# Cross-attention and expert layer on one core: head projections at tiles 4, 6, 8 and 10, the maxima turned at tile 11 behind the scores, the query jobs right behind the last scores

## What is computed

```python
def _L0_xattn_ref(x, context, Wq, Wk, Wv, Wo, bo):      # x (16, 256, 128), context (16, 1601, 96)
    q = (x @ Wq).reshape(B, Nq, HEADS, DIM_HEAD).transpose(0, 2, 1, 3)       # HEADS 16, DIM_HEAD 64
    k = (context @ Wk).reshape(B, Nc, HEADS, DIM_HEAD).transpose(0, 2, 1, 3)
    v = (context @ Wv).reshape(B, Nc, HEADS, DIM_HEAD).transpose(0, 2, 1, 3)
    sim = jnp.einsum('bhid,bhjd->bhij', q, k) * SCALE
    attn = jax.nn.softmax(sim, axis=-1)
    out = jnp.einsum('bhij,bhjd->bhid', attn, v)
    out = out.transpose(0, 2, 1, 3).reshape(B, Nq, HEADS * DIM_HEAD)
    return out @ Wo + bo
...
x = x + _L0_xattn_ref(_layernorm(x, axis=-1), ctx_768, Wq, Wk, Wv, Wo, bo)
x = x + _L0_ffn_ref(_layernorm(x, axis=-1), router, experts, shared expert)
```

## Time and profile before

| what | value |
| --- | --- |
| median of 3 runs | 3302.86 us (3302.56 to 3302.99) |
| the profiled execution | 3302.1 us, of which the trace's span is 3300.3 us |
| TensorE busy | 3269.1 us, 99% of the span |
| VectorE busy | 2383.1 us, 72% |
| ScalarE busy | 1938.2 us, 59% |
| GpSimd busy | 1069.6 us, 32% |
| first scores of the attention, start | 38.19 us |
| first expert matmul, start | 2967.16 us |

### The profile page before, as it was taken

The page is one execution under the profiler, slowest core; times in us unless marked ns, Lnnn a source line. Parts: engine busy times, 40 slices in busy tenths (PEclk is TensorE's granted clock), DMA queues, the critical chain, the costliest instruction groups (busy, mean ns, idle before and its releaser), DMA issues.

```text
span 3300.3 us, 40940 instructions
## 1 busy us (share of the span) xinstructions
PE 3269.1 (99%) x15518; PEld 2606.8 (79%) x15518; DVE 2383.1 (72%) x4915; ACT 1938.2 (59%) x2236; POOL 1069.6 (32%) x710
## 2 busy tenths in 40 slices
PE   8999999999999999999999999999999999999999
PEld 6777777777787777877777777777777877777887
DVE  6777777777777777777777777777777777777655
ACT  4565555655556555665556655566655666575554
POOL 4322233222332233322233222322223322225555
PEclk9999999999999999999999999999999999999999
DMA  2000000000000000000000000000000001000000
GB/s 79 1 16 1 16 1 11 6 1 16 1 16 1 16 1 16 1 1 16 1 16 1 16 1 16 1 9 8 1 16 1 16 1 39 1 3 4 7 7 10
DMA packets 8055, 32.39 MB, mean 10 GB/s; under 512 B 1585, under 2 KB 2354, under 8 KB 7474
## 3 DMA queue, kind: packets, MB, share of 16 engines
q1 hardware_dynamic: 7858, 29.78, 2.9%
HBM read 27.41 MB, written 2.10 MB: 9 GB/s over the span
## 4 chain that ended last, share of the span: by engine, by line
PE 98%; DVE 1%; issue 0%; ACT 0%; DMA 0%; POOL 0%; POOLq 0%; DVEq 0%; ACTq 0%
PE st L529 12%; PE st L532 12%; PE st L535 12%; PE op L543 12%; PE op L549 12%; PE op L546 12%; PE side L475 11%; PE side L555 3%; PE st L636 2%; PE st L638 2%; PE st L637 2%; PE side L468 1%; PE side L470 1%; PE side L469 1%; PE op L636 1%; PE op L637 1%
## 5 line engine op out<-in xcount | busy, mean ns | idle before, releaser
L796 ACT ACTIVATE p_full<-st 128x1024 f32<-128x1024 f32 (+1 forms) x832 | 853.8, 1026 | 1128.5 <-PE st L535 1128.4
L1061 DVE TENSOR_REDUCE m_part<-side 128x1 f32<-128x402 f32 x2016 | 1078.2, 571 | 550.6 <-PE side L475 550.6
L410 POOL TENSOR_TENSOR p_lo<-p_full,p_hi 128x1024 fp32r<-128x1024 f32 x256 | 669.2, 2614 | 2063.7 <-ACT p_hi L799 2063.7
L799 ACT ACTIVATE p_hi<-st 128x1024 fp32r<-128x1024 f32 (+1 forms) x832 | 848.6, 1020 | 0.0
L1049 DVE TENSOR_TENSOR p_lo<-p_full,p_hi 128x1024 fp32r<-128x1024 f32 (+1 forms) x576 | 700.3, 1216 | 132.7 <-ACT p_hi L799 132.7
L475 PE MATMUL side<-cT_hi,qT_hi 96*128 96x402 f32 x2016 | 555.2, 346 | 0.0
L529 PE MATMUL st<-qT_hi,cT_hi 97*128 97x512 f32 (+1 forms) x1664 | 538.4, 405 | 2.3 <-DMA qT_hi<-m_row 2.3
L543 PE MATMUL op<-p_hi,v_hi 128*97 128x512 f32 (+1 forms) x1664 | 527.1, 398 | 0.5 <-DVE p_lo L1049 0.5
L532 PE MATMUL st<-qT_lo,cT_hi 96*128 96x512 f32 (+1 forms) x1664 | 524.8, 397 | 0.0
L535 PE MATMUL st<-qT_hi,cT_lo 96*128 96x512 f32 (+1 forms) x1664 | 521.9, 395 | 0.0
L549 PE MATMUL op<-p_hi,v_lo 128*97 128x512 f32 (+1 forms) x1664 | 521.1, 394 | 0.0
(11 more groups left out here) (164 smaller groups left out, 2606.0 us busy)
## 6 DMA issues: line engine op xcount, KB each, us to landing
keys_nat<-in_ctx_keys SPq DMA_DIRECT2D x16, 624.0 KB, 5.8
keys_tur<-in_ctx_turned SPq DMA_DIRECT2D x16, 603.0 KB, 4.9
gud_raw<-in_moe_w SPq DMA_DIRECT2D x2, 1152.0 KB, 7.8
out_x<-x SPq DMA_DIRECT2D x8, 256.0 KB, 2.0
x<-in_x SPq DMA_DIRECT2D x1, 1920.0 KB, 12.1
qT_hi<-m_row SPq DMA_DIRECT2D x64, 4.0 KB
aw<-in_attn_w SPq DMA_DIRECT2D x2, 448.0 KB, 5.3
aw<-in_attn_w SPq DMA_DIRECT2D x1, 896.0 KB, 9.3
```

What stands on the lines that cost most here:

```text
L410: pool.tensor_tensor(p_lo[:, slot(s), :], p_full[:, s % 2, :], p_hi[:, slot(s), :].bitcast(F32), ALU.subtract).then_inc(s_lo_pool, 1)
L796: act.activation(p_full[0:m, s % 2, :], both(st[0:m, s % 2]), ACT.Exp, scale=SCALE)
L799: act.activation(p_hi[0:m, slot(s), :], both(st[0:m, s % 2]), ACT.Exp, scale=SCALE).then_inc(s_ex, 1)
L1061: dve.tensor_reduce(m_part[:, at:at + 1], where[:, 0:MAXW], AX.X, ALU.max).then_inc(s_drain, 1)
```

## The change

Three Y jobs move away from tile 11. One stands now behind the four M of tile 4, one behind those of tile 6, one behind those of tile 10; the one at tile 8 stays. T moves from behind `pv(9)` to ahead of it, right behind `qk(11)`. The two Q move from behind `pv(10)` to ahead of it, right behind `qk(12)`, and since one table serves all engines, `queries_lo` on VectorE moves ahead of `lo(11)` and `lo(12)`. N moves from tile 6 to tile 7. The numbers of the jobs, and so their banks and wait values, follow from the table. No instruction is added or taken away.

```diff
-        PLACES = {2: ("MM", "M"), 3: ("MM", "M"), 4: ("MM", "MM"), 5: ("MM", "M"), 6: ("MM", "MM"),
-                  7: ("MM", "MM"), 8: ("MM", "MY"), 9: ("MM", "MM"), 10: ("MM", "MM"), 11: ("YY", "YT"),
-                  12: ("", "QQ")}
-        EXTRA = {2: {5: "L", 6: "N"}, 3: {5: "R"}}
+        PLACES = {2: ("MM", "M"), 3: ("MM", "M"), 4: ("MM", "MMY"), 5: ("MM", "M"), 6: ("MM", "MMY"),
+                  7: ("MM", "MM"), 8: ("MM", "MY"), 9: ("MM", "MM"), 10: ("MM", "MMY"), 11: ("T", ""),
+                  12: ("QQ", "")}
+        EXTRA = {2: {5: "L", 7: "N"}, 3: {5: "R"}}
```

## The result

| | median | runs |
| --- | --- | --- |
| before | 3302.71 us | 3298.80 to 3302.99 |
| changed | 3685.10 us | 3675.04 to 3691.81 |

The changed kernel is slower: ratio 1.1158, with a 95% interval from 1.1127 to 1.1190. The forecast was 3592 us in a range of 3555 to 3630, so the direction was right and the size was not: 93 us more came than the forecast, and the time lies outside the range. Its runs also scatter over 17 us, where those of before scatter over 4. The profiled execution took 3691.81 us, of which the span is 3690.0 us.

The account below looks back on a forecast made before the run. TensorE, busy 99% of the span, was taken as the bound, so only new waits count: 132.3 + 5.4 + 151.9 = 289.6 us on the profiled 3302.1 us, giving a median of 3592 us, 8.8% slower, range 3555 to 3630.

Parts of the forecast that it names:

- bank waits: Head projections (Y) behind two M at tiles 4, 6, 10 wait for a bank's drain: 0.70 us each, 132.3 us.
- N: Turn moved from tile 6 to tile 7 starts 0.34 us later behind its M, 16 times: 5.4 us.
- The long wait: TensorE at pv(11) waits for tile 11's remainder, behind the queries' remainders on VectorE: 2.45 us in 62 groups, 151.9 us.
- T: Moved ahead of pv(9) at tile 11: its inputs are ready and its row goes out earlier, so it costs nothing.
- the number of runs of fp32 jobs: Five runs of fp32 jobs end per group instead of three; claimed to cost nothing that the rows show.
- One sign: In the changed trace TensorE's busy time stays near 3269 us while the span grows, its share falling to about 92%.
- the clock falls: Rival, 8%: TensorE's idle piece in each of 62 groups lowers the clock, 2.6 us lost each, 161 us more: 3753 us.
- the rival's dearer case: Clock rival (8%) with 3.4 us instead of 2.6 us lost at each of 62 long waits: 3803 us.
- Not slower: Rival, 2%: head projections find VectorE done, queries' remainder is over in time, N's waits go too: 3292 us, 0.3% faster.
- one wait missing: Rival, 4%: either tile 11's remainder is in time (3441 us) or the third job finds its bank free (3455).
- doesn't do what it says: Rival, 1%: the change doesn't do what it says; the built order was held to show that it does.

Follow-up runs that it names:

- the needless matmuls: Changed kernel plus eight needless 512-column matmuls on TensorE between pv(10) and pv(11), inside the wait for tile 11's remainder: 3596.42 us, ratio 1.0895.
- the copies early: Changed kernel with ScalarE's two copies of the queries ahead of the exponentials of tile 12 instead of behind them: 3534.14 us, ratio 1.0704.

## Why the prediction was wrong

**The waits: right.** That TensorE had no waits to save, and that the change brings 189 bank waits, 16 longer turns and 62 waits for the remainder of tile 11, is what the trace of the changed kernel shows, with these counts. The sum was 289.6 us; with a clock kept up by the needless matmuls it measured 295.

- The bank waits were sized at 0.70 us, the value of the turn, and measured 0.75. The forecast's upper end named the reason: weights of L555 behind the wait take longer to come in than those of L442. 132.3 us became 142.
- N was sized at 0.34 us more, and its idle weight-load time grew by 5.8 us in 16, 0.36 each.
- The long wait was sized at 2.45 us and measured 2.37: 151.9 us became 147. Its chain met each start within 0.02 us.
- T and the number of runs of fp32 jobs cost nothing that could be seen.
- One sign failed without the clock: TensorE's busy time was to stay near 3269 us, but a matmul behind a wait is recorded longer, and with the copies early, where every wait is there and the clock stays up, it is 3332.3 us. The share of "about 92%" would be 91% by the forecast's own numbers (3269 of 3592).

**The step that failed** is the judgement "the clock falls (8%)". Of the 93 us over the forecast 89 are the clock (3685.1 - 3596.4), and the range was closed at 3630 to leave that rival out. Two arguments carried it. The first was that the expert layer kept the clock at 1.00 with 4.1 us of idling in 25. But these were pieces of about a microsecond, like those of the kernel with the copies early, which keeps its clock as well. They say nothing of a piece twice as long. The trace of before had two such pieces, of 2.11 and 2.33 us, one right behind the other at the start of the attention:

```profile
35.58 0.27 PE L479 MATMUL side<-ident,m_neg 128*8 128x128 f32 x1 [2.11 <-DVE m_neg L920]
38.19 1.20 PE L529 MATMUL st<-qT_hi,cT_hi 97*128 97x512 f32 x2 [2.33 <-DMA qT_hi<-m_row]
```

```profile
36.34:38.19 1.85, 0.00 (x1) 0.04 (x1) 0.97 (x2) 0.00 (x0) 0.00 (x0) 0.50 0.01 2
```

The clock fell at 36.34 us, 0.5 us into the second of them, so the idling ahead of the second had its part in it, and it stayed down for 6.8 us (half of that is the 3.4 us of the rival's dearer case). This was the only evidence of the right size, no clean case of a lone piece, and it spoke for the rival. The second argument was that each new piece "stands alone among work without gaps"; the trace shows that this doesn't protect: the clock falls with TensorE busy at full pace on both sides.

The rival as it was priced, 3753 us, was too dear in its turn. It let the clock fall behind each of 62 waits, 2.6 us lost a time. In the profiled execution it fell behind 45, and (3691.8 - 3596.7) / 45 = 2.1 us were lost a time. So the truth lay between the two cases, where the range had nothing. The Trainium skill ("TensorE: Matmul & The Clock Gate", on HAM oscillation) says that idle gaps between bursts send the clock down again and again, once per gap; its example has gaps of 3 to 5 us. The trace agrees as to the kind, and differs in two things: gaps of 2.15 us are enough here, and 45 of 62 brought a fall, not every one.

**Not slower, one wait missing, doesn't do what it says**: none of it came.

## What to carry to other kernels

When a change puts an engine's wait on the matrix engine's path, price the wait and the clock apart, and take the clock's price from idle pieces of the same length; where the trace has none, keep the range open up to it. A job that stands third in a row on two banks waits for the first one's drain, wherever it stands, so put such jobs behind a single fill: here that alone made a kernel 11 us faster, by putting 16 jobs behind one M in place of two. One table that orders all engines moves the waits of each of them; what the moving engine gains nothing by, another may pay for, and its order can be kept apart.

## What the runs showed of the hardware

- Needless work can pay: 496 matmuls put into idle time made a kernel 89 us faster, by keeping the clock on its upper level.
- The clock falls between 0.2 us before TensorE resumes and 1.5 us after, so the loss shows as longer matmuls, not as idle time. Of the 159 us by which TensorE's busy time grew with the same instructions, the clock made 96 (3428.0 against 3332.3 us in the kernel with the copies early, which has every wait, the long ones shortened, and no fall). The other 63 are matmuls that are recorded longer behind waits. L529 took 427 ns on average in the changed kernel, 411 with the waits and the clock up, 405 before.
- Idle pieces of 1.15 us, 62 of them, never brought it down; of 1.7 us 22 did, of 2.15 us 45 or 48, and which of them follows from where on an even raster of times each ends. Once down it stayed for 3.4 us mostly, sometimes for 10.2.
- Behind a wait, four fp32 matmuls with their weights took 0.47 us in place of 0.36, and a first pair of 512 columns 0.54 in place of 0.46.
